# Storing the y hats of a unit in DRAM once and not twice, in a deformable convolution kernel on one core

## The reference

```python
x = x + _L0_conv_ref(_gn(x), ...)
x = x + _L1_conv_ref(_gn(x), L1_conv_w_off, L1_conv_b_off, L1_conv_w_def)
# _L1_conv_ref: x = relu(x); K = 3
offset = conv(x, w_off) + b_off            # 2 offsets for each of 9 taps and each pixel
py, px = base_y + off[:, :, 0], base_x + off[:, :, 1]
samp = _bilinear_gather(x, py, px)         # zero outside the image
out = einsum('bckhw,ock->bohw', samp, w_def)
```

## Time and profile before

| what | value |
|---|---|
| median of 3 runs | 1555.24 us (1554.58 to 1559.01) |
| the profiled execution, its own time | 1554.93 us |
| its span, from the first to the last instruction | 1553.1 us |
| mean granted clock of PE | 0.98 |
| DMA traffic | 268.12 MB in 190711 packets |

### The profile page before, as it was taken

One profiled execution on the slowest core, in us unless ns is written; L12 is line 12 of the kernel. 1 busy time (PEld: TensorE's weight loads), 2 busy tenths in 40 slices (PEclk: granted clock), 3 DMA queues, 4 the chain that ended last, 5 costly groups with the idle time before them and its releaser, 6 DMA issues.

```text
span 1553.1 us, 28171 instructions
## 1 busy us (share of the span) xinstructions
PE 1475.3 (95%) x9363; PEld 987.8 (64%) x9364; DVE 1057.3 (68%) x2155; ACT 1036.0 (67%) x1884; POOL 1006.9 (65%) x627
## 2 busy tenths in 40 slices
PE   4999999964999999999999999999999999999997
PEld 3777777742566666666666666666666666666664
DVE  4988888863666666666666666666666666666664
ACT  2555555535777777777777777777777777777762
POOL 3555555634777667777776677777667777766671
PEclk9999999975999999999999999999999999999999
DMA  4333433334666666666666666666666676666660
GB/s 134 111 113 116 120 112 112 105 123 127 191 196 202 200 196 200 196 198 200 203 193 198 198 200 199 201 193 199 197 192 200 184 211 203 200 191 201 184 175 29
DMA packets 190711, 268.12 MB, mean 173 GB/s; under 512 B 19810, under 2 KB 128382, under 8 KB 190590
## 3 DMA queue, kind: packets, MB, share of 16 engines
q1 hardware_dynamic: 190590, 266.60, 58.8%
HBM read 188.33 MB, written 78.18 MB: 172 GB/s over the span
## 4 chain that ended last, share of the span: by engine, by line
PE 74%; SPq 1%; DMA 1%; POOL 1%; DVE 0%; ACT 0%; issue 0%; POOLq 0%; DVEq 0%
PE bank L854 33%; PE pair L822 24%; PE pair L870 7%; PE pair L899 7%; PE pair L837 2%; POOL weights L1681 1%; DMA hat_x<-hats 0%; SPq L628 0%; DMA hx_all<-hat_x 0%; SPq L611 0%; SPq L617 0%; ACT dist L1073 0%; SPq L632 0%; DVE hats L1377 0%; POOL offs_parts L1692 0%
## 5 line engine op out<-in xcount | busy, mean ns | idle before, releaser
L1681 POOL TENSOR_TENSOR weights<-hy_all,hx_all 112x768 f32<-112x768 f32 x384 | 746.9, 1979 | 324.8 <-PE bank L854 303.3
L1392 DVE SCALAR_TENSOR_TENSOR samples_lo<-bank,samples_hi 128x288 f16<-128x288 f32 (+1 forms) x1024 | 452.5, 462 | 356.9 <-ACT samples_hi L1080 351.3
L854 PE MATMUL bank<-weights,zT 112*128 112x288 f32 (+1 forms) x2176 | 597.0, 403 | 0.3 <-DVE samples_lo L1392 0.3
L1080 ACT ACTIVATE samples_hi<-bank 128x288 f16<-128x288 f32 (+1 forms) x1024 | 393.7, 418 | 205.6 <-PE bank L854 189.0
L854 PEld LDWEIGHTS bank<-weights,zT 112*128 112x128 f32 x2176 | 380.9, 190 | 132.0 <-DVE samples_lo L1392 28.9
L822 PE MATMUL pair<-samples_hi,w_hi 128*128 128x512 f16 x576 | 218.9, 380 | 1.3 <-DVE samples_lo L1392 1.3
L822 PE MATMUL pair<-samples_lo,w_hi 128*128 128x512 f16 x576 | 217.6, 378 | 0.0
L822 PE MATMUL pair<-samples_hi,w_lo 128*128 128x512 f16 x576 | 217.4, 377 | 0.0
L870 PE MATMUL pair<-ident,z 128*112 128x128 f32 x1088 | 172.3, 273 | 3.3 <-DVE zT L1412 2.6
L870 PEld LDWEIGHTS pair<-ident,z 128*112 128x112 f32 x1088 | 133.1, 134 | 59.3 <-DVE zT L1412 3.3
L1588 POOL TENSOR_TENSOR samples_lo<-samples_hi,samples_lo 128x512 f16<-128x512 f32 x64 | 74.2, 1159 | 126.1 <-ACT samples_lo L985 126.0
(11 more groups left out here) (142 smaller groups left out, 1774.1 us busy)
## 6 DMA issues: line engine op xcount, KB each, us to landing
hy_all<-hat_y SPq DMA_DIRECT2D x384, 192.0 KB
hx_all<-hat_x SPq DMA_DIRECT2D x384, 192.0 KB
hat_y<-hats SPq DMA_DIRECT2D x256, 126.0 KB
raw<-x_pad SPq DMA_DIRECT2D x68, 272.0 KB, 4.6
x_pad<-hy_all SPq DMA_DIRECT2D x64, 272.0 KB, 3.4
weights<-in_x SPq DMA_DIRECT2D x64, 256.0 KB, 3.0
out<-y SPq DMA_DIRECT2D x32, 512.0 KB, 3.6
hat_x<-hats SPq DMA_DIRECT2D x128, 72.0 KB
```

The costliest lines, as they stand in the source:

```text
L854: mm = nc.tensor.matmul(sampled_step(n, p)[:, :, c0 - first:c1 - first], zT[0:WPIX, u * WINDOWS + w, :], weights[0:WPIX, u, :, c0:c1], sta ...
L1080: nc.scalar.activation(samples_hi[:, u, :, c0:c1], sampled_step(n, p), ACT.Copy).then_inc(samples_ready, 1)
L1392: nc.vector.scalar_tensor_tensor(out=samples_lo[:, u, :, c0:c1], in0=sampled_step(n, p), scalar=1.0, in1=samples_hi[:, u, :, c0:c1], op0=A ...
L1681: nc.gpsimd.tensor_tensor(to, hy_all[0:WPIX, i * TROWS:(i + 1) * TROWS, :], hx_all[0:WPIX, i * TROWS:(i + 1) * TROWS, :], ALU.mult).then_i ...
```

## The change

One constant is changed. The rows of `hat_y` for each tap row fall from 28 to 14, the loop over copies in `store_hats` runs once, and `spread_hats` reads each of 8 DRAM rows 8 times instead of each of 16 rows 4 times. `hats_landed` waits for 4 transfers and no longer for 6.

```diff
--- before.py
+++ after.py
-COPIES = 2
+COPIES = 1
```

## The result

| | kernel before | changed kernel |
|---|---|---|
| median, same chip | 1554.62 us (1552.96 to 1559.01, 20 runs) | 1559.63 us (1555.06 to 1569.36, 20 runs) |
| ratio, 95% interval | | 1.004 [1.0027, 1.0053] |
| profiled execution, its own time | 1554.93 us | 1558.82 us |
| its span | 1553.1 us | 1557.0 us |

The kernel became slower, by 0.4% where 5.8% was forecast: +5 us and not +91. The sign was right and the size was not, and the reason for the size fell with it: the DMA loop did become longer, but in the profiled execution it did not take over from PE. The 20 times of the changed kernel lie further apart than those before: six of them are 1564.9 to 1569.4 us, the other fourteen 1555.1 to 1560.6. None of the six was profiled, so what follows on the whole stage holds for the execution of 1558.82 us.

A forecast was written before the change was run, and what follows sets the result against it. PE bounds the kernel at 18.20 us a unit; the DMA loop was to take over at 19.6. First spread 362.5 + 63 x 19.6 + 21.0 + 26.2 = 1644.5, plus 1.8 around the span: 1646 us (+5.8%), range 1551 to 1715.

The forecast's parts named there:

- What bounds the kernel, and the second loop behind it: Second stage: PE sets the pace at 18.20 us a unit; behind it a DMA loop of stores and spread turns in 16.64.
- Which engines work: Spread of hats: hy falls from 16 to 8 DMA engines; the loaded eight carry 96 packets a unit instead of 72.
- Two of six stores go: Stores of a unit: 1.7 us less SP issue, first spread at 362.5 not 364.15; store data 2.4 to 1.5 us a turn.
- The spread on eight engines: Spread of a unit: 96 packets at 167 ns take 16.0 us, near today's price of 172 ns.
- The loop after: DMA loop: 1.8 idle, 16.0 spread, 1.5 stores, 0.3 out and raw transfers make 19.6 us a turn, above PE's 18.20.
- The threshold of 152 ns: Spread's packet price at which the formula meets today's span, a turn of 18.15 us; below it, no slowdown.
- The end: Last unit: 21.0 us from spread issue to last product, then 26.2 us; span is 409.7 + 63 x turn.
- What waits then: POOL waits long for hat_in, with offs_parts and PE's locate behind it; PE would idle 1.4 of 19.6 us.
- No slower: Rival: eight engines run at 129 ns, turn 16.0 us, PE stays the bound, 1553 us; 0.17 together with the y-transfer rival.
- The destination alone: Rival: partitions written set the price, three pieces at 188 ns, three at 129; turn 18.8 us, 1596 us; chance 0.25.
- The y transfer keeps 16 engines: Rival: hy's 64 partitions count, not its source rows; turn 15.7 us, 1553 us; 0.17 together with the no-slower rival.
- eight engines get in each other's way: Rival: reading one DRAM row eight times in step costs 188 ns or more; turn 21.6 us, 1772 us; chance 0.05.

The follow-up runs named there:

- light kernels: Kernels before and changed, two of three convolution products left out: 1480.18 and 1561.26 us; with all pieces written to partitions 32 to 111: 1480.43 and 1495.32 us.
- light changed kernel: Changed kernel with two of the three products of the second stage's convolution left out, so PE needs less: 1561.26 us, mean turn 18.38 us.
- the upper partitions: Changed kernel with all six pieces of a spread written to partitions 32 to 111: 1554.26 us, ratio 0.9995 to the kernel before.
- the half landings: Changed kernel with a landing semaphore for each half of the columns: 1553.73 us (0.9987 to the kernel before), on a second chip 1556.99 us (1.0009).

## Why the prediction was wrong

*What bounds the kernel, and the second loop behind it:* right. With PE out of the way the kernel before turns in 16.99 us; I had read 16.64 from its first turns. The wait for the hats in the earlier trace rows is not the loop's slack, as I had it: it stayed at 165.5 us.

*Which engines work:* right, by 28 and 48 small packets less and a busy share near half. The Trainium skill (DMA: Bandwidth & Descriptors, Rules for kernel authors) says that such a transfer is confined; the trace agrees, with 16 small packets a piece. What that costs is another matter, and stands two steps down.

*Two of six stores go:* right in kind. The turn outside the spread fell by 0.7 us in the light kernels (4.6 to 3.9), where my terms give 0.6 (4.2 to 3.6), and the first spread came 3.0 us earlier, not 1.7.

*The spread on eight engines:* **this step failed.** I put 96 packets at 167 ns, 16.0 us. The light changed kernel takes 14.5 us, 151 ns. The late packets cost 132 ns, much as in the earlier trace rows; the early ones were put too high. I had kept today's price because the writes to partitions 0 to 79 stay, and took off only a little for the other eight engines, which no longer compete. The counts show that this is worth more: an early packet fell from 194 to 163 ns as the engines at work went from about twelve to eight, and from 183 to 138 where every piece goes to the same partitions. The partitions are the other part: on eight engines, 163 to 138 ns. So the 172 and 188 ns were prices beside other engines at work and could not be carried over to eight alone. The earlier trace rows hinted at it: 197 GB/s at 75.6% of sixteen engines, twelve at work, and 200 at 52.4%, eight; but there the partitions change as well.

*The loop after:* 1.8 + 14.5 + 1.5 + 0.3 would have been 18.1; 18.36 and 18.38 were measured, against 19.6 forecast. The threshold of 152 ns was about right, and the kernel stands on it. That the forecast had the sign right is therefore partly luck: the two edits that shorten the turn, the upper partitions and the half landings, bring the time back to within 0.15% of the kernel before.

*The end:* the form held. With measured turns it gives 1482, 1569, 1483 and 1500 us in the light kernels, where 1480, 1561, 1480 and 1495 were measured. But the sum holds only while the turn is longer than PE's unit. In the profiled execution it is not (18.15 against 18.20 us), so no difference adds up over 63 turns, and only the first units pay.

*What waits then:* POOL's wait, with offs_parts and PE's locate behind it, is as described, but only in the first units (PE 10.8 against 7.8 us).

*The rivals.* "No slower" had the outcome for the long stage, with a wrong price: 129 ns holds for late pieces only. It also missed that the fill of the pipeline has no slack, which turned its gain of 2.3 us into a loss of 4. "The destination alone" had the right kind of price, slow early pieces and fast late ones on eight engines, and was nearest in the turn (18.8 us); its 188 ns was again taken beside other engines at work. The Trainium skill (SBUF — State Buffer, Door 1: The DMA port swizzle) has low partitions reach half the ports; the trace agrees on eight engines (50 against 58 packets per us, in the light kernels) and shows little of it with twelve at work (61 against 63). "The y transfer keeps 16 engines" is out by the marks, "eight engines get in each other's way" by the early price, 163 ns and not 188 or more.

## What to carry to other kernels

The time of a packet, read from a trace, holds for the engines at work then and the partitions written then. Moved to fewer engines, a transfer costs less than in proportion where packets get faster as engines drop out: here a third more packets on the loaded engines (72 to 96) made the spread 17% longer (12.4 to 14.5 us). Before a price is carried over, look for two stretches that differ in the number of engines alone, or in the partitions alone. A loop hidden behind another engine is measured by taking work from that engine; in the whole kernel its length does not show until it is too late. And a loop that ends within 1% of the bound is a result that the next chip or the next edit can tip (0.4%, 1.6%, 0.1% here).

## What was not expected of the hardware

Eight DMA engines started 81% as many 3 KB packets per us as about twelve did early in a spread (49.8 against 61.3, light kernels): two thirds of the engines, but 163 ns a packet and not 194. Partitions 32 to 111 instead of 0 to 79 gave eight engines 16% more packets (49.8 to 57.6), and twelve at work 3% (61.3 to 63.2). The spread's early part moved 188 GB/s on the mean, 77 packets per us (238 GB/s) at its best, though the loads of raw moved 300; what holds it there was not found.
